# The second MLP's second layer as sign weights in float32r, with its own place in the order

## The chip, the cores and the metric

The kernel runs on one core of a Trainium2 chip. The metric is the device time of one execution in microseconds. The median of three runs before the change is 4103.9 us (4095.98 to 4111.07).

## The reference, cut to what matters

A two-layer transformer block works on `x` of 8 x 1024 x 256. The first layer has a windowed attention, a routed "heavy" attention and a small MLP; the second has a causal attention of 16 heads and an MLP with two-valued weights. The changed part is that last MLP, whose weights are replaced by their signs times a mean per output row:

```
def _binarize(w):
    alpha = jax.lax.stop_gradient(jnp.mean(jnp.abs(w), axis=1, keepdims=True))
    bw = alpha * jnp.sign(w)
    return w + jax.lax.stop_gradient(bw - w)
bw1 = _binarize(w1)                                   # 1024 x 256
h = jnp.einsum('bsd,hd->bsh', x, bw1) + b1
h = jax.nn.gelu(h, approximate=False)
bw2 = _binarize(w2)                                   # 256 x 1024
out = jnp.einsum('bsh,dh->bsd', h, bw2) + b2
```

Around it: `h = layernorm(x) * (1 + cb) + sb`, and `x = x + gb * out`.

## The kernel before, in words

The work goes batch by batch (`b`, 8 of them), and most stages by halves of a batch (`c`, 512 of the 1024 tokens). Each stage is written as a Python generator on each engine, and one list, `ORDER`, says whose step comes next; all engines follow that same list, each issuing its own instructions in order. `schedule()` makes the list from three lanes. Lane 0 holds `light` (windowed attention: 17 or 12 steps of QKV projections, then two steps for each of 16 units, and a tail) and `att` (the causal attention). Lane 1 holds `chain`, `heavy` and `mlp1`, lane 2 the other chains, `hrows` (row gathers for the heavy attention) and `hnorm`. `PACE` says how many steps of lane 0 go into one round, `SIDE` how many of a side lane, the constants after it (`HROWS_BEHIND_MLP` and so on) where a stage may begin, and `LAG` holds back `hnorm` and the first two chains.

`mlp1(b, c)` has 24 steps. Steps 0 to 7 are `norm_half`: statistics and normalisation on VectorE, a transposition on TensorE (L1471), and the split of the normalised input into two float32r parts, `hT2h` (ScalarE, L2322) and `hT2l`, the rest (VectorE, L1945). Steps 8 to 15 are the first layer, one block `m` of 128 hidden rows a step: two input blocks times two parts are four float32r matmuls of 512 columns against signs `w1s` (L1710, L1711), and ScalarE applies GELU with the block's mean `alpha1` as scale (L2442) into `g1`. Steps 16 to 23 are the second layer: for each of four token tiles, eight float32 matmuls with a tile of `g1` as stationary operand and `w2T` (256 columns) as moving one (L1724). Each of these float32 matmuls is two instructions in the trace. VectorE then multiplies by the gate (L2167) and GpSimd adds into `xt` (L2667). The signs of `w2` are multiplied by their means in the setup (VectorE and GpSimd).

First halves (`c = 0`) run beside the first steps of `att(b, 1)`, whose fills (L1568 to L1578 on TensorE) VectorE reduces (L2070 to L2078), and beside `hrows(b + 1)` (gathers L2501 on GpSimd, L1820 on VectorE). Second halves (`c = 1`) run beside `light(b + 1, 0)`, but for the last, which runs alone. In `light`, L1283 and L1287 are the QKV projections, L1774 and L2223 the masked scores and the exponentials, L1320 the turning of a unit. `exp_tables()` reloads ScalarE's table before an exponential when a GELU has been before it (L2180).

The lines that count most for the order:

```
if key[0] == "mlp1" and key[2] == 0 and n == 1 and not reached([(("att", key[1], 0), steps_of(("att", key[1], 0)))]):
    return
MLP1_BANKS = {0: (6, 7), 1: (7, 5, 6)}
```

## Time and profile before

| what | value |
|---|---|
| median of three runs | 4103.9 us |
| the profiled execution, its own time | 4090.72 us |
| its span, first to last instruction | 4089.0 us |
| TensorE busy | 3394.9 us, 83% |
| VectorE, ScalarE, GpSimd busy | 60%, 48%, 36% |
| mean granted TensorE clock | 0.911 |

The span is the stretch that the rows of the trace cover; the execution's own time has 1.7 us around it. Durations below are those of this execution, which lies 13.2 us under the median of the runs. An engine's busy share is taken over the whole span, in which stages with different limits follow each other eight times. A matmul's duration contains its latency, so the spacing of starts tells more than the mean duration.

### The profile page before, as it was taken

The numbers are of one execution on the slowest core, as the hardware profiler recorded it, in microseconds if no ns is written. First come the engines' busy times: TensorE is split into PE (matmuls) and PEld (weight loads), VectorE is DVE, ScalarE is ACT, GpSimd is POOL, SyncE is SP. The second block draws the span as 40 slices with busy tenths as digits, with TensorE's granted clock in tenths as the row PEclk, the third lists the DMA queues.
The fourth block names the chain that finished last, engine by engine and source line by source line (L and its number), as shares of the span: only waits on it lengthen the run. The fifth ranks groups of instructions, "written<-read, shape, count | busy, mean of one in ns | idle before, by whom it ended". The sixth has DMA issues, their size and how long they took to land. (4 is left out here: it accounts for less than half of the span.)

```text
span 4089.0 us, 81864 instructions
## 1 busy us (share of the span) xinstructions
PE 3394.9 (83%) x30905; PEld 2029.7 (50%) x30905; DVE 2463.2 (60%) x6188; ACT 1955.4 (48%) x4555; POOL 1478.4 (36%) x1799
## 2 busy tenths in 40 slices
PE   6368778897799878997798987998788977999787
PEld 2235554564446544565445544465444644456444
DVE  6755657367563666547573676637674465836662
ACT  5124445554364544554355543654445543655534
POOL 4123442244323542234422443235422344225411
PEclk8579789998899989998899988999899988999888
DMA  6210230002300122002400013002310024000220
GB/s 236 81 37 14 55 105 28 14 24 53 110 16 25 44 70 73 16 12 59 112 18 14 28 48 110 17 24 55 83 49 16 12 60 113 15 22 20 64 68 7
DMA packets 233604, 207.39 MB, mean 51 GB/s; under 512 B 13777, under 2 KB 214225, under 8 KB 233177
## 3 DMA queue, kind: packets, MB, share of 16 engines
q1 hardware_dynamic: 229168, 192.61, 16.7%
q0 software_dynamic: 3328, 8.39, 0.8%
q8 instruction: 252, 4.13, 0.4%
q14 instruction: 136, 1.11, 0.1%
q10 hardware_dynamic: 720, 1.15, 0.1%
HBM read 123.83 MB, written 77.69 MB: 49 GB/s over the span
## 5 line engine op out<-in xcount | busy, mean ns | idle before, releaser
L2399 ACT ACTIVATE arena<-pb 128x512 f32<-128x512 f32 (+3 forms) x1536 | 664.6, 492 | 239.5 <-PE pb L1615 232.2
L2479 POOL TENSOR_TENSOR arena<-arena,small 128x512 f32<-128x512 f32 x256 | 286.5, 1122 | 456.0 <-DVE small L1791 454.6
L2223 ACT ACTIVATE arena<-arena,small 128x256 f32<-128x256 f32 x512 | 255.8, 500 | 387.3 <-DVE small L1774 386.9
L1573 PE MATMUL pb<-arena 96*32 96x128 bf16 (+5 forms) x5280 | 372.4, 280 | 57.8 <-DVE arena L2078 23.7
L1615 PE MATMUL pb<-arena 98*32 98x512 bf16 (+3 forms) x4608 | 396.3, 339 | 28.1 <-ACT arena L2399 20.2
L1633 PE MATMUL pb<-arena,v 128*17 128x512 f32 (+3 forms) x3072 | 382.0, 499 | 24.1 <-POOL arena L2643 15.0
L2078 DVE TENSOR_REDUCE arena<-pb 128x1 f32<-128x512 f32 x512 | 333.1, 685 | 83.7 <-PE pb L1573 82.3
L2643 POOL TENSOR_SCALAR_AFFINE_SELECT arena<-arena 128x256 f32<-128x256 f32 x512 | 216.3, 426 | 461.1 <-ACT arena L2399 457.7
L1774 DVE CUSTOM_DVE_ANT_0 arena<-pb,wmask 128x256 f32<-128x256 f32 x512 | 195.8, 419 | 214.2 <-PE pb L1310 205.5
L1573 PEld LDWEIGHTS pb<-arena 96*32 96x32 bf16 (+1 forms) x5280 | 185.5, 102 | 246.9 <-issue 71.3
L1310 PE MATMUL pb<-arena 128*128 128x256 f32 x1024 | 280.3, 398 | 4.8 <-issue 3.6
L1287 PE MATMUL pb<-hTf,wqkv 128*128 128x512 f32 (+1 forms) x640 | 246.7, 537 | 24.4 <-DVE hTf L1743 11.5
L1724 PE MATMUL pb<-w2T,arena 128*128 128x256 f32 x1024 | 244.5, 391 | 10.8 <-ACT arena L2442 10.8
L1615 PEld LDWEIGHTS pb<-arena 98*32 98x32 bf16 x4608 | 138.5, 96 | 204.8 <-ACT arena L2399 108.6
L2349 ACT ACTIVATE arena<-arena,cols 128x256 f32<-128x256 f32 x256 | 148.5, 595 | 159.9 <-DVE arena L1988 158.1
L2070 DVE TENSOR_REDUCE arena<-pb 128x4 f32<-128x512 f32 x256 | 171.6, 688 | 84.9 <-PE pb L1573 82.4
L1724 PEld LDWEIGHTS pb<-w2T,arena 128*128 128x128 f32 x1024 | 196.6, 196 | 46.2 <-ACT arena L2442 14.5
L1310 PEld LDWEIGHTS pb<-arena 128*128 128x128 f32 x1024 | 187.1, 194 | 57.7 <-issue 26.1
L1320 PE MATMUL pb<-ident,arena 128*128 128x128 f32 x1024 | 161.4, 281 | 55.7 <-DVE arena L1784 34.3
L2539 POOL TENSOR_TENSOR arena<-arena,small 128x256 f32<-128x256 f32 x128 | 78.5, 613 | 348.2 <-DVE small L1886 348.1
L1578 PE MATMUL pb<-cmask,identb 128*32 128x512 bf16 (+1 forms) x640 | 120.0, 414 | 92.2 <-DMA arena<-split_k 56.0
L2072 DVE TENSOR_REDUCE arena<-pb 128x2 f32<-128x512 f32 x256 | 169.6, 686 | 26.8 <-PE pb L1573 26.4
(339 smaller groups left out, 7137.2 us busy)
## 6 DMA issues: line engine op xcount, KB each, us to landing
arena<-split_q SPq DMA_DIRECT2D x64, 384.0 KB, 3.8
arena<-split_k SPq DMA_DIRECT2D x24, 768.0 KB, 6.6
split_q<-arena SPq DMA_DIRECT2D x64, 192.0 KB, 2.1
split_q<-arena SPq DMA_DIRECT2D x96, 128.0 KB, 1.9
split_k<-arena SPq DMA_DIRECT2D x64, 192.0 KB, 2.2
split_k<-arena SPq DMA_DIRECT2D x96, 128.0 KB, 1.9
arena<-split_k SPq DMA_DIRECT2D x24, 384.0 KB, 8.2
xn<-h_d SPq DMA_DIRECT2D x8, 1024.0 KB, 9.3
```

Of the source, the lines that this page charges most:

```text
L1287: mm = t.matmul(bank[bk][:, 0:hi - lo], wqkv[:, k, col0:col0 + P], hT[:, k, lo:hi], start=k == 0, stop=k == KD - 1)
L1310: mm = t.matmul(bank[bk][:, j * 2 * P:(j + 1) * 2 * P], qt[:, p_, j, i * P:(i + 1) * P], kt[:, p_, i * P:i * P + 2 * P], start=True, stop= ...
L1573: mm = t.matmul(out[r:r + wide], qh[:, q0 + r:q0 + r + wide], kh_, **kw)
L1615: mm = t.matmul(bank[bk][r:r + 32, 0:w_], ka[slot(c, g)][0:KA, h, kt_ * P + r:kt_ * P + r + 32], qa[slot(c, g)][0:KA, h, q0:NH], start=Tru ...
L1633: t.matmul(bank[3][32 * h:32 * h + HD1 + 1, q0:NH], v1[:, kt_, G1 * g + h, :], pp[pn % 4][:, h % 2, 0:w_], start=kt_ == 0, stop=kt_ >= TH ...
L1724: mm = t.matmul(bank[bk][:, 0:D], g1[:, k, i * P:(i + 1) * P], w2T[:, k], start=k == 0, stop=k == FT - 1)
L1774: ins = v.tensor_tensor_reduce(out=sm[n % 2][:, j], in0=bank[n % 2][:, j * 2 * P:(j + 1) * 2 * P], in1=mk, scale=-1.0, scalar=3e38, op0=AL ...
L2078: ins = v.tensor_reduce(m[:, h, i, 3:4], bk, AX_X, ALU.max)
L2223: ins = s.activation(pm[n % 3][:, j], sm[n % 2][:, j], ACT.Exp, bias=nmx[:, 2 * sl + j:2 * sl + j + 1], scale=-1.0, accum_out=sml[:, 2 * s ...
L2399: s.activation(pp[pn % 4][:, h % 2, 0:w_], bank[n % 3][:, 0:w_], ACT.Exp).then_inc(a_exp1, 1)
L2479: g.tensor_tensor(pm[n % 3], pm[n % 3], rcl[:, 2 * sl:2 * sl + 2].unsqueeze(2).broadcast_to([P, 2, 2 * P]), ALU.mult).then_inc(p_norm0, 1)
L2643: g.affine_select(out=p2, in_=p2, pattern=[[0, 2], [1, P]], compare_op=ALU.is_ge, fill=0.0, base=0, channel_multiplier=-1).then_inc(p_tri, 1)
```

## The change

The second layer is computed like the first: signs as stationary operand in float32r, the activations as moving operand in two parts. GELU writes `gt`, two buffers of one block; VectorE copies it to float32r (`gh`) and subtracts the copy from it (`gl`). For each block `k` and each half `d` of the outputs there are two matmuls of 512 columns into two banks that collect all eight blocks (`MLP1_SUM`), so the output comes out transposed. ScalarE takes it out with the mean as scale (`moT`), TensorE turns it back by eight transpositions into two banks (`MLP1_TURN`), and VectorE's gate product and GpSimd's addition work on two token tiles at once. The second layer of block `m - 2` stands in the same step as the first layer of block `m`: after it in first halves, ahead of it in second halves. First-layer outputs of second halves have one bank (7) where there were three. The stage still has 24 steps. In the setup the signs of `w2` are no longer multiplied by their means. The order's constants change: `PACE`, `SIDE`, `HROWS_BEHIND_MLP`, `LAG`.

```
-PACE = {("light", 0): (1.88, 0.9, 0.9), ("light", 1): (1.0, 1.463, 1.1), ("att", 0): (1.461, 0.9, 0.9, 0.72), ("att", 1): (1.0, 1.15, 1.15, 0.632)}
+PACE = {("light", 0): (1.311, 0.9, 0.9), ("light", 1): (1.0, 1.463, 1.1), ("att", 0): (1.461, 0.9, 0.9, 0.72), ("att", 1): (1.0, 1.15, 1.15, 0.507)}
-        ("mlp1", 0): 1.0, ("mlp1", 1): 0.98, ("hrows", 0): 1.0, ("hnorm", 0): 1.0}
+        ("mlp1", 0): 0.99, ("mlp1", 1): 1.684, ("hrows", 0): 1.0, ("hnorm", 0): 1.0}
-HROWS_BEHIND_MLP, HEAVY_BEHIND_HROWS, HEAVY_BEHIND_ATT, HNORM_BEHIND_ATT, ATT_BEHIND_MLP, MLP_BEHIND_LIGHT = (6, 12, 11, 45, 13, 2)
+HROWS_BEHIND_MLP, HEAVY_BEHIND_HROWS, HEAVY_BEHIND_ATT, HNORM_BEHIND_ATT, ATT_BEHIND_MLP, MLP_BEHIND_LIGHT = (10, 12, 11, 45, 13, 2)
-LAG = 11
+LAG = 16
...
-                        v.wait_ge(b_alpha, 2 * m + 2)
-                        v.wait_ge(r_h[0], 16 * 2)
-                        v.scalar_tensor_tensor(out=wtmp[m % 2][:, 0:width], in0=sgn[:, c0:c0 + width], scalar=ac, in1=w, op0=ALU.mult,
-                                               op1=ALU.subtract).then_inc(b_sign, 1)
+                        v.tensor_copy(w, sgn[:, c0:c0 + width]).then_inc(b_add, 1)
                         yield
...
-                    g.wait_ge(b_sign, m - FT + 1)
-                    g.tensor_tensor(w, w, wtmp[m % 2][:, 0:width], ALU.add).then_inc(b_add, 1)
...
-        MLP1_BANKS = {0: (6, 7), 1: (7, 5, 6)}
+        MLP1_NORM, MLP1_W1, MLP1_SUM, MLP1_TURN = ({0: (6, 7), 1: (7, 5)}, {0: (6, 7), 1: (7,)}, {0: (0, 1), 1: (5, 6)}, {0: (6, 7), 1: (7, 5)})
...
+                    def second(k):
+                        if k == 0:
+                            for bk in sums:
+                                for w in left[bk]:
+                                    t.wait_ge(*w)
+                                left[bk] = None
+                        t.wait_ge(gl_set, FT * H + k + 1)
+                        for d in range(KD):
+                            t.matmul(bank[sums[d]], w2s[:, k, d * P:(d + 1) * P], gh[:, k % 3], start=k == 0, stop=False)
+                            mm = t.matmul(bank[sums[d]], w2s[:, k, d * P:(d + 1) * P], gl[:, k % 3], start=False, stop=k == FT - 1)
+                        mm.then_inc(t_w2, 1)
+
+                    for m in range(FT + 2):
+                        if m < FT and c == 0:
+                            first(m)
+                        if m >= 2:
+                            second(m - 2)
+                        if m < FT and c == 1:
+                            first(m)
+                        yield
+                    for d in range(KD):
+                        left[sums[d]] = [(a_mo, KD * H + d + 1)]
+                    yield
+                    for u in range(2):
+                        bk = MLP1_TURN[c][u]
                         for w in left[bk]:
                             t.wait_ge(*w)
-                        for k in range(FT):
-                            if i == 0:
-                                t.wait_ge(a_g, FT * H + k + 1)
-                            mm = t.matmul(bank[bk][:, 0:D], g1[:, k, i * P:(i + 1) * P], w2T[:, k], start=k == 0, stop=k == FT - 1)
...
+                        t.wait_ge(a_mo, KD * H + KD)
+                        for i in range(2):
+                            for d in range(KD):
+                                mm = t.transpose(bank[bk][:, (KD * i + d) * P:(KD * i + d + 1) * P], moT[:, d, (2 * u + i) * P:(2 * u + i + 1) * P], ident[:, :])
+                        mm.then_inc(t_mo, 1)
...
+                    for m in range(FT + 2):
+                        k = m - 1
+                        if 0 <= k < FT:
+                            v.wait_ge(a_g, FT * H + k + 1)
+                            if k >= 3:
+                                v.wait_ge(t_w2, FT * H + k - 2)
+                            v.tensor_copy(gh[:, k % 3], gt[:, k % 2]).then_inc(gh_set, 1)
+                        if 0 <= k < FT:
+                            v.wait_ge(gh_set, FT * H + k + 1)
...
+                            v.tensor_tensor(gl[:, k % 3], gt[:, k % 2], gh[:, k % 3].bitcast(F32), ALU.subtract).then_inc(gl_set, 1)
+                        yield
...
+                        v.tensor_tensor(xadd2[u], bank[MLP1_TURN[c][u]].rearrange("p (t d) -> p t d", t=2), gates[:, 3].unsqueeze(1).broadcast_to([P, 2, D]),
+                                        ALU.mult).then_inc(v_w2, 1)
...
+                            s.wait_ge(t_w1, FT * H + m + 1)
+                            if m >= 2:
+                                s.wait_ge(gl_set, FT * H + m - 1)
+                            gelu_tables[0] = True
+                            s.activation(gt[:, m % 2], bank[MLP1_W1[c][m % len(MLP1_W1[c])]], ACT.Gelu, scale=alpha[:, m:m + 1],
+                                         bias=cols[:, C_FB1 + m:C_FB1 + m + 1]).then_inc(a_g, 1)
+                        yield
+                    s.wait_ge(t_w2, FT * (H + 1))
+                    s.wait_ge(gl_set, FT * (H + 1))
+                    for d in range(KD):
+                        s.activation(moT[:, d], bank[MLP1_SUM[c][d]], ACT.Copy, scale=alpha[:, FT + d:FT + d + 1]).then_inc(a_mo, 1)
```

## Rows read from the trace of the kernel before

**Rows 1.** The page's part 1: busy us, share of the span, instructions of each engine.
```profile
PE 3394.9 (83%) x30905; PEld 2029.7 (50%) x30905; DVE 2463.2 (60%) x6188; ACT 1955.4 (48%) x4555; POOL 1478.4 (36%) x1799
```

**Rows 2.** Groups by line and form, TensorE: count, busy us, mean ns, idle before.
```profile
L1724 PE MATMUL pb<-w2T,arena 128*128 128x256 f32 x1024 | 244.5, 391 | 10.8 <-ACT arena L2442 10.8
```

**Rows 3.** Windows, a first half: length, busy PE, PEld, DVE, ACT, POOL, PEclk, DMA.
```profile
1526.00:1563.00 37.00, 30.98 (x134) 23.54 (x135) 14.69 (x34) 9.44 (x12) 16.07 (x16) 0.84 0.68 181
```

**Rows 4.** Windows: a second half, and the mean over all seven.
```profile
1724.00:1771.00 47.00, 42.15 (x191) 30.90 (x190) 11.92 (x45) 30.95 (x54) 8.41 (x9) 0.96 0.00 1
...
sum 322.00, PE 288.53 PEld 213.62 DVE 83.11 ACT 199.23 POOL 58.72; mean PE 41.22 PEld 30.52 DVE 11.87 ACT 28.46 POOL 8.39
```

**Rows 5.** Waits of TensorE in the first half, 1526 to 1563 us.
```profile
PE pb L1471 <- DVE arena L1933: 6.3, 1, 6.3
PE pb L1578 <- DVE arena L2070: 2.5, 1, 2.5
PE pb L1710 <- DVE hT2l L1945: 2.3, 1, 2.3
```

**Rows 6.** Waits of TensorE in the second half, 1724 to 1771 us.
```profile
PE pb L1710 <- ACT arena L2442: 2.4, 2, 1.8
PE pb L1724 <- ACT arena L2442: 2.4, 1, 2.4
```

**Rows 7.** Timeline of the first half: gathers, their readers, second layer's first two tiles.
```profile
1528.97 1.08 POOL L2501 DMA_INDIRECT arena<-h_d,idx_all  x1 [3.79 <-PE pb L1471]
...
1544.22 0.42 DVE L1820 CUSTOM_DVE_ANT_0 arena<-arena 128x256 f32<-128x256 f32 x1 [4.34 <-DMA arena<-h_d,idx_all]
...
1546.56 4.54 PE L1724 MATMUL pb<-w2T,arena 128*128 128x256 f32 x16
...
1551.38 3.62 PE L1724 MATMUL pb<-w2T,arena 128*128 128x256 f32 x16
```

**Rows 8.** Timeline of the second half: a table load and what waits behind it.
```profile
1737.26 1.28 ACT L2442 ACT_TABLE_LOAD   x1
...
1738.55 1.45 ACT L2442 ACTIVATE arena<-pb,cols,alpha 128x512 f32<-128x512 f32 x2
1739.38 0.65 PE L1710 MATMUL pb<-hT2h,w1T 128*128 128x512 f32 x1 [1.83 <-ACT arena L2442]
```

**Rows 9.** ScalarE's groups by line and form: GELU's and exponentials' table loads.
```profile
L2442 ACT ACT_TABLE_LOAD x38 | 48.8, 1283 | 24.1 <-PE pb L1711 23.6
L2180 ACT ACT_TABLE_LOAD x37 | 47.5, 1283 | 60.2 <-PE pb L1615 34.2 <-DVE small L1879 25.5
L2232 ACT ACTIVATE arena<-pb 128x512 f32<-128x512 f32 x128 | 74.0, 578 | 60.5 <-PE pb L1320 60.5
```

**Rows 10.** Timeline of the last half, full clock: starts of neighbouring float32r matmuls; second layer.
```profile
4061.44 0.39 PE L1711 MATMUL pb<-hT2l,w1T 128*128 128x512 f32 x1
4061.67 0.40 PE L1710 MATMUL pb<-hT2h,w1T 128*128 128x512 f32 x1
...
4065.01 14.08 PE L1724 MATMUL pb<-w2T,arena 128*128 128x256 f32 x64
```

**Rows 11.** Timeline: eight transpositions of 128x128 float32 in a row.
```profile
1711.13 1.04 PE L1260 MATMUL pb<-ident,xn 128*128 128x128 f32 x8
```

**Rows 12.** VectorE's groups by line and form.
```profile
L2078 DVE TENSOR_REDUCE arena<-pb 128x1 f32<-128x512 f32 x512 | 333.1, 685 | 83.7 <-PE pb L1573 82.3
L2167 DVE TENSOR_TENSOR arena<-pb,gates 128x256 f32<-128x256 f32 x64 | 27.2, 425 | 170.8 <-PE pb L1724 138.3 <-issue 32.6
L1945 DVE TENSOR_TENSOR hT2l<-arena,hT2h 128x512 fp32r<-128x512 f32 x32 | 22.5, 707 | 1.4
L1992 DVE TENSOR_TENSOR arena<-pb,gates 128x512 f32<-128x512 f32 x32 | 22.1, 692 | 37.7 <-PE pb L1512 37.7
L845 DVE CAST arena<-arena 128x256 f32<-128x256 bf16 x8 | 2.3, 288 | 0.0
L994 DVE COPY arena<-arena 128x128 f32<-128x128 f32 x1 | 0.2, 218 | 0.0
```

110 lines of the change are left out of this document (49 added, 61 removed).

## The prediction

> **What bounds the kernel now.** I read the page's busy shares first: TensorE is busy 83% of the span, VectorE 60%, ScalarE 48%, GpSimd 36% [rows 1]. No engine is full, but TensorE is the one to which stages come back, so work taken off it counts where it is the last wait. Then I looked where the changed stage stands. It appears in 16 clusters: eight first halves of some 37 us beside the first fills of the causal attention, seven second halves of some 46 us beside the next batch's QKV projections and first attention units, and one second half alone at the end. The windows show that they are bounded differently. In a first half TensorE is busy 31.0 of 37 us, VectorE only 14.7, and the granted clock is 0.84 [rows 3]: part of it runs at 1.2 GHz, behind a 6.3 us wait for the norm [rows 5]. In the second halves TensorE is busy 288.5 of 322 us and ScalarE 199.2 [rows 4].
>
> The waits name what the rest is. In a first half TensorE waits 2.3 us for the split of the input and 2.5 us in a fill for VectorE [rows 5]; VectorE itself then stood in its queue before a gather's landing (4.34 us, L1820) [rows 7]. In a second half both waits of 2.4 us go to the GELU [rows 6], and the timeline shows why: GELUs alternate with the attention's exponentials, each change loads a table for 1.28 us, and TensorE stands 1.83 us for the bank behind it [rows 8]. Both loads together are there 75 times [rows 9], some 8 in each of the seven second halves.
>
> **The change: array work.** The old second layer is 64 instructions a half (1024 over 16 halves [rows 2]), 14.08 us at 2.4 GHz, so 0.22 us each [rows 10]. The new one is 8 blocks x 2 outputs x 2 parts = 32 float32r matmuls of 512 columns. The first layer has that form already; neighbouring ones start 0.23 us apart [rows 10], so 7.4 us. The eight transpositions of the result cost 1.0 us [rows 11]. Net -5.7 us a half, at full clock.
>
> **VectorE and ScalarE.** Eight subtractions a half are like L1945, 0.71 us [rows 12]. The copy of 128x512 float32 to float32r in SBUF is not in the trace. Copies inside SBUF took 0.218 us for 128 elements and 0.288 for 256 [rows 12]; that line gives 0.43 at 512. The other bound is one element a cycle like the subtraction, 0.71. I take 0.43, since the nearest rows are copies too. Four gate products of 0.425 become two of 0.692 [rows 12]. VectorE gets 8 x 1.14 + 1.4 - 1.7 = 8.8 us more a half (11 with the dear copy), 141 us in all, 60% to 63 or 64%. ScalarE takes out two banks more, 0.58 us each [rows 9].
>
> The Trainium skill (SBUF — State Buffer, on the port pair that VectorE and GpSimd share) says that such a copy locks the pair and that GpSimd cannot write a gather's descriptors meanwhile. No row here shows that lock; it speaks against the change, and it is a rival below.
>
> **First halves.** A step of both layers is 8 matmuls, 1.86 us, and a fill of about 0.5 us beside it; VectorE has 0.43 + 0.71 + 0.69 for the fill's reduction [rows 12], 1.83 us, and 2.3 in the steps with a gathered row. So TensorE still ends last, barely. Worked out with the new constants, the order has `hrows` begin four mlp steps later, and its readers on VectorE at mlp steps 14 to 17 and not 10 to 13, while GpSimd still issues the gathers right behind its bias addition. They have landed then, so the 2.5 us wait goes, and with it the dip of the clock behind it: the first tile at L1724 took 4.54 us, the next 3.62 [rows 7], so 0.9. What is late next: second(0) waits for GELU, copy and subtraction of block 0 (1.0 us after the steps at hand), VectorE and TensorE share the pace for eight steps (0.2 each, 1.6), and the transpositions wait for `moT` (0.9, ScalarE's two copies less the fills between). Sum: -5.7 - 2.5 - 0.9 + 3.5 = -5.6 us. Bounds -7.5 (no new wait) and -2.5 (the dear copy and a wait of 0.6 us in each step). `heavy` still begins after attention step 11, and VectorE's scaling of the gathered rows is done just before, which I cost at nothing; if late it is 1 us.
>
> **Second halves.** By the order all eight GELUs now stand beside QKV steps 8 to 15, whose evacuations need no exponential. So no alternation: the 4.8 us of waits go [rows 6], and the 1.9 us that a clock of 0.96 takes out of 47 us [rows 4]. With the array work that is -12.4 us. Back come these. The norm's steps are pressed between QKV steps 2 and 7, so the split is late by 1.2 us (its 2.3 us chain [rows 5] less the QKV step that covers it). First-layer blocks 0 and 1 follow each other with one bank and no second layer between: one table load and one GELU, 1.28 + 0.78, and the semaphores, 2.3 us [rows 8]. In later steps TensorE's second(m - 1), 0.93 us, covers GELU(m - 1), 0.78 with its semaphores, but for 0.1; 1.0 in all. `moT` stands on ScalarE behind the evacuation of QKV step 16, which waits for TensorE, while TensorE is already at the transpositions: 0.2 + 0.6 + 1.2 = 2.0 us. Behind these transpositions on TensorE stands `light` step 17, so the attention units wait as well. Last, the first attention units lose the mlp matmuls that covered their softmax: 1.2 us. Sum of these 7.7, net -4.7 us. Bounds: -9 (half of them hidden) and -1.5 (1 us in each of three more steps).
>
> The Trainium skill (ScalarE: Activation LUTs, what a table load costs) has 2.66 us for a switch, with a drain. Here the GELU starts 1.29 us after the load [rows 8], so the trace decides; by the page the one bubble would be 1.4 us longer in each second half, some 10 us in all.
>
> **The last half** is alone. With one bank a step is first layer, GELU, next first layer: 0.93 + 0.78 + 0.3 = 2.0 us, 16 for eight, where it was 7.5 + 14.1 = 21.6 behind each other, and its tail is longer by 4 us: -1.5 us (+2 to -3). The setup loses two small products on VectorE and two on GpSimd beside the token selection; I cost it at nothing. `LAG` 16 moves the first two chains and every `hnorm` by a few steps; `hnorm` now ends at attention step 70 of 77, some 8 us of TensorE's work before it is needed, which covers it.
>
> **Sum.** 8 x -5.6 = -45, 7 x -4.7 = -33, -1.5: -79 us against the execution of 4090.7, so 4012, a factor of 0.981. On the median of 4103.9 it is 4025.
>
> **The rivals.**
> - More comes: the new waits mostly hide, -7.5 and -9 a half: 8 x 7.5 + 7 x 9 + 3 = 126, so 3978. For it speaks that the profile shows slack on ScalarE; against, that a queue in program order rarely hides all.
> - VectorE sets the pace: the dear copy and steps of 2.6 us in first halves, the chain late in second ones: 8 x 2.5 + 7 x 1.5 - 2 = 28, so 4075.
> - GpSimd is locked out (the skill's rule as a mechanism here): each pair of copy and subtraction, 1.1 us, can hold back one of the four gathers, up to 4.5 us, and the readers stall VectorE's queue with the copies behind it. Half of the first halves' gain goes: +22 us, 4047. The wait of 4.34 us [rows 7] speaks for a sore spot, the four steps' delay against it.
> - No change: what TensorE gains in the halves is waited for at `heavy` and the chains, where VectorE ends last. Within 20 us of 4104. Little speaks for it, as nothing there depends on a fixed time.
> - Slower, by one mechanism: one step's links run in series, because VectorE's copy stands behind an evacuation that waits for TensorE. Then a step in second halves is 0.93 + 1.0 + 0.43 + 0.71 + 0.93 = 4.0 us for 1.86, +21 us a half for the -12.4 gained. In second halves alone that is 7 x 21 - 7 x 12.4 - 45 = +15; in first halves too, whose gain without new waits is 9.1 us, it is 15 x 21 - 87 - 73 = +155. I put it between, +85, at 4189. It decides from (87 + 45) / 70 = 1.9 us of wait in each step of second halves. Against it: second(m - 2) lies two steps behind its first layer.
>
> **Chances.** My forecast 0.56 (own range 4000 to 4052), more 0.14, GpSimd 0.09, VectorE 0.10, no change 0.05, slower 0.06. The range for 8 in 10 is 3985 to 4075: it leaves out the lower part of "more", and the last two. Half a per cent, about 20 us, is what a measurement can tell from no change. Faster 0.89, same 0.05, slower 0.06.
>
> **What would show it.** In the profile after: L1724's group gone, the new float32r pair at 0.23 us spacing; the SBUF copy at 0.43 us; table loads down from 77 to some 33; no gather wait on VectorE in first halves; first halves near 30.5 us; TensorE busy some 90 us less, VectorE some 140 more; a wait of about 2 us before the second halves' transpositions. Wrong would be: copies of 0.7 us, TensorE waiting for `gl` in most steps, or halves that are shorter while the time between them grows.

## The result, and the profile after

The changed kernel takes 4079.28 us (median; 4075.96 to 4080.89) beside 4095.98 us (4087.93 to 4111.07) for the kernel before in the same comparison: a ratio of 0.994, with a 95% interval of 0.9921 to 0.9958. A second measurement (e1) gave 0.9932 (0.991 to 0.9954). It is faster, but by 17 to 27 us where 79 were forecast, and it lies just outside the forecast's range of 3985 to 4075.

The page of the changed kernel, its head and part 1 (busy us, share of the span, instructions):

```profile
span 4075.6 us, 81566 instructions
...
PE 3334.5 (82%) x30521; PEld 1944.0 (48%) x30521; DVE 2603.0 (64%) x6412; ACT 1924.3 (47%) x4543; POOL 1470.0 (36%) x1765
```

Against [rows 1] VectorE has 139.8 us more, as forecast (141). TensorE's busy time fell by 60 us where some 90 had been forecast; what became of the rest stands below the table. The prices of the new layer's single instructions are right. Groups of the changed kernel by line and form (VectorE: subtraction, copy, gate product, scaled gathered rows; TensorE: the second layer's pair; ScalarE: the table loads before GELUs and before exponentials):

```profile
L2179 DVE TENSOR_TENSOR gl<-arena,gh 128x512 fp32r<-128x512 f32 x128 | 94.4, 738 | 4.4
L2174 DVE CAST gh<-arena 128x512 fp32r<-128x512 f32 x128 | 55.2, 432 | 120.7 <-ACT arena L2470 107.3 <-issue 13.0
L2188 DVE TENSOR_TENSOR arena<-pb,gates 128x512 f32<-128x512 f32 x32 | 21.3, 682 | 11.0 <-PE pb L1736 11.0
L1843 DVE TENSOR_SCALAR arena<-arena,small 128x256 f32<-128x256 f32 x32 | 18.0, 567 | 0.3
...
L1714 PE MATMUL pb<-gh,w2T 128*128 128x512 f32 x256 | 118.2, 462 | 7.2 <-DVE gl L2179 6.8
L1715 PE MATMUL pb<-gl,w2T 128*128 128x512 f32 x256 | 104.3, 407 | 0.0
...
L2470 ACT ACT_TABLE_LOAD x16 | 20.5, 1283 | 40.4 <-PE pb L1702 40.4
L2204 ACT ACT_TABLE_LOAD x15 | 19.2, 1283 | 63.2 <-PE pb L1606 24.0 <-DVE small L1890 22.9 <-DVE small L1785 16.2
```

The copy takes 0.432 us (0.43 taken), the subtraction 0.738 (0.71). With two loads in the setup there are 33 table loads (33 forecast; 77 before [rows 9]). GELUs no longer alternate with exponentials.

So the pieces are as forecast, and the time isn't. To see where it went I cut every batch at the same four instructions in both traces: **second-half stretch**, from the next batch's first transposition to its 13th attention unit; **untouched stretch**, from there to the norm's first transposition of the first half, in which no changed instruction stands; **first-half stretch**, from there to the first score of `att(b, 1)`'s heads, so the mlp with what follows it, `heavy`'s beginning; and the rest of the batch. Sums over the profiled executions, in us; e3 is an experiment below, the kernel before with nothing changed but the order's constants:

| stretch | before | e3 | after | forecast for the change | measured |
|---|---|---|---|---|---|
| up to batch 0's first transposition | 236.1 | 235.8 | 231.9 | 0 | -4.2 |
| batch 0 without its first half | 441.0 | 436.8 | 437.1 | 0 | -3.9 |
| eight first-half stretches | 588.7 | 569.5 | 572.7 | -45 | -16.0 |
| seven second-half stretches | 567.9 | 559.2 | 557.8 | -33 | -10.1 |
| seven untouched stretches | 1512.4 | 1529.3 | 1528.6 | 0 | +16.2 |
| seven rests | 693.7 | 693.3 | 695.1 | 0 | +1.4 |
| last half | 49.3 | 49.0 | 52.4 | -1.5 | +3.1 |
| span | 4089.0 | 4072.9 | 4075.6 | -79 | -13.4 |

The profiled execution of the kernel before (4090.7 us) lies below the median of its runs in every comparison (4096 to 4106), so the table shows 13.4 of the 17 to 27 us. A part of that is in the untouched stretches, which are as short as 1512.4 us in no other trace (e6, below).

Windows over the seven first-half stretches of batches 1 to 7, the sum line (length, busy us of each engine, mean of one), first of the kernel before:

```profile
sum 511.90, PE 417.47 PEld 236.40 DVE 292.01 ACT 133.51 POOL 148.24; mean PE 59.64 PEld 33.77 DVE 41.72 ACT 19.07 POOL 21.18
```

The same of e3, the old layer in the new order:

```profile
sum 494.42, PE 410.39 PEld 231.50 DVE 290.82 ACT 133.51 POOL 145.84; mean PE 58.63 PEld 33.07 DVE 41.55 ACT 19.07 POOL 20.83
```

The same of the changed kernel:

```profile
sum 497.36, PE 387.85 PEld 197.05 DVE 358.77 ACT 142.56 POOL 144.46; mean PE 55.41 PEld 28.15 DVE 51.25 ACT 20.37 POOL 20.64
```

From e3 to after, TensorE's busy time falls by 3.2 us a half and its idle time grows by 3.6 (length less busy: 70.6 - 58.6 = 12.0, then 71.1 - 55.4 = 15.6). The same happens in the seven second-half stretches: busy 73.7 to 69.9, idle 6.2 to 9.8. The busy time that the new layer takes off TensorE comes back as waiting, and it is less than the 5.7 us forecast. Two second-half stretches with the full clock throughout (1.00) show how much less; batch 3 of e3, then batch 2 of the changed kernel (length, busy of PE, PEld, DVE, ACT, POOL, granted clock, DMA share, GB/s):

```profile
1699.99:1775.84 75.85, 72.15 (x345) 49.44 (x344) 27.99 (x97) 33.20 (x77) 24.01 (x25) 1.00 0.10 32
1216.12:1293.24 77.12, 67.91 (x322) 43.77 (x320) 36.52 (x111) 34.61 (x79) 23.64 (x23) 1.00 0.10 32
```

That is 4.2 us and not 5.7: without the second layer's own matmuls TensorE's busy time in these two is 59.0 and 60.6 us, so the other ones show 1.6 us more. Why isn't shown. The rest of what is missing is the clock: of a first-half stretch 11.6 us are lost to it in e3 and 14.4 after (length times what the mean granted clock lacks to 1).

The waits of TensorE in one first-half stretch (batch 2; us in total, times, longest), before; those for the norm and the split are in [rows 5]:

```profile
PE pb L1578 <- DVE arena L2070: 3.1, 2, 2.5
PE pb L1573 <- DVE arena L2078: 3.0, 2, 2.8
```

The second of these in e3 (L1578 is down to 0.6 there):

```profile
PE pb L1573 <- DVE arena L2078: 3.3, 2, 2.8
```

And in the changed kernel, where L1578 is L1569 and L1573 is L1564:

```profile
PE pb L1462 <- DVE arena L1944: 6.3, 1, 6.3
PE pb L1564 <- DVE arena L2089: 5.4, 3, 2.3
...
PE pb L1701 <- DVE hT2l L1956: 2.4, 1, 2.4
PE pb L1736 <- ACT arena L2476: 1.0, 1, 1.0
PE pb L1569 <- DVE arena L2081: 0.6, 1, 0.6
```

The 2.5 us wait behind the gather is gone, as forecast (L1578 3.1 to L1569 0.6), and e3 shows that the order did that. But the other wait for the fills' reductions grew from 3.0, and 3.3 in e3, to 5.4, so that TensorE waits for reductions as long as before, 6.0 us for 6.1. VectorE's timeline there, in the changed kernel (start, us, line, operation), shows what they stand behind:

```profile
1546.30 0.68 DVE L2188 TENSOR_TENSOR arena<-pb,gates 128x512 f32<-128x512 f32 x1
1546.90 0.26 DVE L1840 TENSOR_SCALAR small<-small 128x4 f32<-128x4 f32 x1
1547.19 1.31 DVE L1843 TENSOR_SCALAR arena<-arena,small 128x256 f32<-128x256 f32 x1
1548.42 0.68 DVE L2089 TENSOR_REDUCE arena<-pb 128x1 f32<-128x512 f32 x1
...
1550.97 0.91 DVE L1851 MEMSET arena<- 64x1024 f32 x1 [0.16 <-issue]
1552.14 0.91 DVE L1852 MEMSET arena<- 64x1024 f32 x1 [0.25 <-issue]
```

A gate product, the norm of the gathered rows and a scaled row stand in VectorE's queue ahead of a reduction (L2089 at 1548.42), for which TensorE waits 2.3 us. It waits 0.8 us for the reduction before it (1545.70), which stands behind the other gate product, and 2.2 us behind `heavy`'s two memsets. Only the first two waits are new: before, the scaled rows and all gate products but the last lay beside the old second layer, in which VectorE waited for TensorE, but the memsets stood behind it then too, with a wait of 2.8 us. Two rows of VectorE's timeline before, a gate product with the idle time ahead of it in brackets, and the first memset:

```profile
1562.81 0.42 DVE L2167 TENSOR_TENSOR arena<-pb,gates 128x256 f32<-128x256 f32 x1 [2.27 <-PE pb L1724]
...
1564.36 0.91 DVE L1840 MEMSET arena<- 64x1024 f32 x1 [0.53 <-issue]
```

### The profile page after: what moved, and what is told of

The parts are those of the page before. It is cut to its first block and busy times, and to the rows that moved or that the text cites. A ratio compares the mean times of both kernels' runs of the same rounds, so it can differ in the third digit from the quotient of the medians.

```text
span 4075.6 us, 81566 instructions
## 1 busy us (share of the span) xinstructions
PE 3334.5 (82%) x30521; PEld 1944.0 (48%) x30521; DVE 2603.0 (64%) x6412; ACT 1924.3 (47%) x4543; POOL 1470.0 (36%) x1765
## 3 DMA queue, kind: packets, MB, share of 16 engines
q1 hardware_dynamic: 229168, 192.61, 16.9%
## 5 line engine op out<-in xcount | busy, mean ns | idle before, releaser
L1564 PE MATMUL pb<-arena 96*32 96x128 bf16 (+5 forms) x5280 | 381.3, 280 | 78.1 <-DVE arena L2089 41.8
L2089 DVE TENSOR_REDUCE arena<-pb 128x1 f32<-128x512 f32 x512 | 335.4, 684 | 94.1 <-PE pb L1564 91.6
L1564 PEld LDWEIGHTS pb<-arena 96*32 96x32 bf16 (+1 forms) x5280 | 184.9, 101 | 273.9 <-DVE arena L2089 84.9
L1278 PE MATMUL pb<-hTf,wqkv 128*128 128x512 f32 (+1 forms) x640 | 258.8, 551 | 30.8 <-DVE hTf L1754 19.1
L1278 PEld LDWEIGHTS pb<-hTf,wqkv 128*128 128x128 f32 x640 | 117.9, 200 | 145.7 <-issue 121.0
L1569 PE MATMUL pb<-cmask,identb 128*32 128x512 bf16 (+1 forms) x640 | 119.4, 412 | 77.8 <-DMA arena<-split_k 59.6
L1311 PEld LDWEIGHTS pb<-ident,arena 128*128 128x128 f32 x1024 | 118.9, 142 | 130.8 <-ACT arena L2256 54.5
```

What stands on the lines that cost most here:

```text
L1278: mm = t.matmul(bank[bk][:, 0:hi - lo], wqkv[:, k, col0:col0 + P], hT[:, k, lo:hi], start=k == 0, stop=k == KD - 1)
L1311: mm = t.transpose(bank[2][:, j * P:(j + 1) * P], pm[n % 3][:, j // 2, (j % 2) * P:(j % 2 + 1) * P], ident[:, :])
L1564: mm = t.matmul(out[r:r + wide], qh[:, q0 + r:q0 + r + wide], kh_, **kw)
L2089: ins = v.tensor_reduce(m[:, h, i, 3:4], bk, AX_X, ALU.max)
```

## The experiments

Each ratio is to the kernel before, with its 95% interval; the changed kernel for comparison is e1 (0.9932). "Stretches" are those of the table, as means of batches 1 to 7.

**e1, the changed kernel again.** No edit.

> The changed kernel once more, as the base of this group and to see how far one stretch differs between two executions of the same program. Theory V (the gain of the first halves is given back to VectorE's queue at their end, that of the second halves to new waits on ScalarE): the stretch from the norm's transpositions to the first attention score is again 71 us and the one from the next batch's first transposition to its 13th attention unit 79.7 us on average, each within 1 us. Theory C (the loss is a chance of TensorE's clock in that one execution): these means move by 2 us or more. The ratio to the kernel before is 0.994.

Measured: 4075.14 us, 0.9932 (0.991 to 0.9954). Its stretches repeat those of the table within 0.5 us each (first halves 71.4 for 71.1, second 79.2 for 79.7, untouched 218.0 for 218.4, means of seven), as theory V had it. Where an experiment below leaves a kind of stretch alone, its mean lies between 70.8 and 71.4 us in first halves and between 79.2 and 80.2 in second ones; a difference inside these bounds says nothing.

### Order and layer apart

**e2, the new layer in the old order.** **e3, the old layer in the new order.**

```
e2: -PACE = {("light", 0): (1.311, ...  +PACE = {("light", 0): (1.88, ...   (all the constants back)
e3: the same constants, the other way, in the kernel before
```

> The new layer in the old order: PACE, SIDE, HROWS_BEHIND_MLP and LAG as they were. Theory V: the layer alone gives the second halves nothing, because GELUs and exponentials alternate again, and with them VectorE's copies; some 10 table loads a half return, so some 25 us slower than the changed kernel, near 4100. Rival (the order is what costs, by pressing the steps together): faster than the changed kernel, 4060 or less.

> The kernel before with the new order's constants alone (PACE, SIDE, HROWS_BEHIND_MLP, LAG); its second layer stays float32. Theory: a good part of what the change gained in second halves is the order's, since it puts all eight GELUs beside QKV steps, so that they no longer alternate with exponentials. That is worth up to 4.8 us a half, 34 us; the shifts in the stretch that holds no instruction of the change cost 2.3 us a batch, 16; the start gains 9, and the last half has nothing of it. Sum -27: about 0.993 to 0.996 of the kernel before. Rival: this order only suits the new layer's steps (in it the old second layer's 14 us stand beside the units of attention, which wait behind them): slower than before by 0.3% or more, and the change's gain is the layer's.

Measured: e2 4124.66 us, 1.0052 (1.0035 to 1.0069): slower than before. Theory V's direction came, at twice its size: it has 77 table loads again, and its second-half stretches are 86.5 us (81.1 before, 79.7 after). e3 4075.16 us, 0.9927 (0.9907 to 0.9946): the same as the whole change. This is the main finding. The new layer alone is a loss of half a per cent in the old order, the order alone is the whole gain, and beside the new order the layer is worth nothing that can be measured. e3's expectation named the direction and, nearly, the size.

The table above then splits the change. The order gives 19.2 us in the first halves, 8.6 in the second ones, and takes 16.9 in the untouched stretches. The layer gives 3.9 in the setup, where its products of signs and means are gone, 1.4 in the second halves, and costs 3.2 in the first and 3.4 in the last (and 1.4 in the parts between: 2.7 in all). Each number is one execution against another; how far the one on the untouched stretches holds is e6's question.

**e6, the old order for the untouched stretch alone**, in the changed kernel.

```
+ for b in range(1, B):
+     (a, z) = places of light(b, 0) step 41 and of mlp1(b, 0) step 1
+     out[a:z] = older[a:z]
```

> The changed kernel with the old order from attention unit 12 of light(b, 0) to the start of mlp1(b, 0), for b from 1 to 7; there no instruction of the change stands, only the order differs by single steps. That stretch is 216.1 us before and 218.4 after on average. Theory O (the new constants shift the chains by a step there, and that costs 2.3 us a batch): back to 216 us, some 14 us less in all, ratio 0.990. Rival (it is TensorE's clock, which falls differently when what comes before has another length): the stretch stays at 218 us and the time within 5 us of the changed kernel, ratio 0.993.

Measured: 4070.91 us, 0.9921 (0.9899 to 0.9944); the interval overlaps e1's. Batch by batch the untouched stretches are 219.5, 214.9, 217.4, 217.4, 213.1, 219.4, 215.4 us, with the kernel before at 217.0, 214.5, 217.4, 218.9, 212.9, 219.2, 212.6 and the changed one at 215.8, 221.6, 219.8, 215.5, 214.5, 216.2, 225.1. The new constants move the steps of the untouched stretch too, and by this pair 11.5 of its 16.2 us come back with the old places. The other traces make it less. Thirteen kernels here have the new places with nothing added there (after, e1, e3, e4, e5, e7, e9, e10, e11, e13, e14, e15, e17), and the seven stretches sum to 1519.8 to 1529.3 us, 1523.6 in the mean; five have the old places (before, e2, e6, e12, e18), with 1512.4 to 1524.2, 1518.9 in the mean. So the new places cost some 5 us, and the 16.2 of the table is mostly a short execution beside a long one. In single batches the places are clear: batch 7 takes 221.0 to 226.0 us with the new ones and 212.5 to 215.5 with the old, batch 2 217.5 to 221.8 and 214.5 to 216.0, but batch 6 213.3 to 217.3 and 218.1 to 220.0.

### What holds the first halves

**e4 and e5, less work for TensorE**: the matmuls on `gl` left out, in first halves (e4) or second halves (e5). The low part of the activations is then missing from the output.

```
-  t.matmul(..., gh[:, k % 3], start=k == 0, stop=False)
-  mm = t.matmul(..., gl[:, k % 3], start=False, stop=k == FT - 1)
+  mm = t.matmul(..., gh[:, k % 3], start=k == 0, stop=k == FT - 1)
```

> In first halves the 16 matmuls with the second part (gl) are left out, VectorE's copy and subtraction stay. 3.7 us of TensorE's work less in each of eight halves. Theory V: VectorE's queue ends the stretch, so less than 1.5 us a half, 0 to 12 us in all. Rival (TensorE still bounds the first halves): 3.5 us a half, 28 us in all.

> In second halves the 16 matmuls with the second part (gl) are left out, VectorE's work stays. Theory V: TensorE bounds these halves but for a few fixed waits, so most of the 3.7 us comes, 20 to 26 us over the seven halves beside the projections. Rival (the chain of GELU, copy and subtraction paces the steps): under 8 us.

Measured: e4 4062.08 us, 0.9903 (0.9883 to 0.9924); e5 4065.66 us, 0.9906 (0.9884 to 0.9929). 16 matmuls of 0.23 us are 3.7 us a half. Of them 1.6 arrived in the first-half stretches (71.05 to 69.47) and 1.35 in the second (79.69 to 78.34), between the two theories in both. Some 40% of the work that was taken off arrived, where the sum had all of it on the path. What became of the rest differs. In first halves it isn't waited for: TensorE's idle time is 15.6 us as in the changed kernel, but 16.9 us are lost to the clock and not 14.4. In second halves idle time grew by 0.8 us and the loss to the clock by 1.0.

**e7, ScalarE makes the copies to `gh` in first halves**, VectorE the subtractions only.

```
+ if c == 0:
+     s.activation(gh[:, m % 3], gt[:, m % 2], ACT.Copy).then_inc(gh_set, 1)
```

> In first halves ScalarE makes the copy gh, right behind each GELU, and VectorE only the subtraction: 8 x 0.43 = 3.4 us less on VectorE. Theory V (VectorE's queue ends the first halves): 1.5 to 3 us a half, 12 to 24 us in all, ratio 0.988 to 0.990. Theory K (TensorE's clock takes back what is gained): under 1 us a half, with more of the half at the lower clock.

Measured: 4069.74 us, 0.992 (0.9897 to 0.9943). VectorE has 4.0 us less in a first-half stretch, and the stretch is 0.6 shorter (70.44). That is theory K's size without its reason, since 13.8 us are lost to the clock beside 14.4.

**e14, less work for VectorE**: the subtraction cut to two columns, both matmuls of a pair read `gh`. **e15, both**: that subtraction, and no second matmul. Both leave out the low part.

```
-  v.tensor_tensor(gl[:, k % 3], gt[:, k % 2], gh[:, k % 3].bitcast(F32), ALU.subtract)
+  v.tensor_tensor(gl[:, k % 3, 0:2], gt[:, k % 2, 0:2], gh[:, k % 3, 0:2].bitcast(F32), ALU.subtract)
```

> The changed kernel with VectorE's subtraction cut to two columns and both matmuls of a pair reading gh (left out: the low part of the activations). TensorE's work is unchanged, VectorE has 5.2 us less in each half, 83 in all. Theory A, VectorE's queue took TensorE's place: 2 to 3 us less in each half, 4037 (0.984 of the kernel before). Theory B, TensorE and its clock set the halves: under 0.7 us a half, 4067 to 4077. Removing TensorE's 3.7 us instead gave 1.6 us a first half and 1.4 a second one (e4, e5).

> The changed kernel without the subtraction (as e14) and without the matmuls on the low part (as e4 and e5 together), so VectorE has 83 us less and TensorE 56 us less. Theory A, the two queues guard each other (either one alone gives back what the other loses): more than e4 + e5 + e14 together, so 4077 - 13 - 10 - 40 - 15, about 4000 or less. Theory B, something outside the layer's own work sets the halves (the norm's chain ahead of them, the readers of the gathered rows, the clock): less than e4 + e5 + e14 together, 4030 to 4050.

Measured: e14 4070.06 us, 0.9905 (0.9882 to 0.9927); e15 4029.13 us, 0.9805 (0.9781 to 0.983). In e14 the first-half stretches are as long as before the edit (71.02 for 71.05) though VectorE has 4.7 us less in each: TensorE's idle time fell by 0.7 us, and 0.8 more were lost to the clock. In e15 they are 67.48, that is -3.6, where e4 alone gave -1.6 and e14 nothing. By the ratios e15 takes 52 us less than e1 (0.9932 - 0.9805, of 4100), and e4, e5 and e14 together 34. The intervals are too wide to prove the difference from the totals; e15's first-half stretch is shorter than e4's in six of the seven batches. That is more than the sum of the parts, as theory A wants it, though the time is the one that theory B named (4030 to 4050). But the reason of theory A, that each queue guards the other, isn't in the trace: TensorE's idle time in a first-half stretch is 15.3 us in e15 and 15.6 in e4 and in the changed kernel. What e15 has beyond e4 is the clock, with 14.8 us lost to it beside 16.9. Why it was higher isn't shown. And the 5.4 us wait for the reductions is still there; TensorE's waits in e15's first-half stretch of batch 2:

```profile
PE pb L1462 <- DVE arena L1943: 6.3, 1, 6.3
PE pb L1564 <- DVE arena L2088: 5.4, 3, 2.3
```

So that wait isn't made by the layer's copies and subtractions. It belongs to the work that now follows the mlp, as e9 shows.

**e9, the old place of the gathered rows** (`HROWS_BEHIND_MLP` 6 and not 10, in the changed kernel).

> HROWS_BEHIND_MLP back to 6 alone, so the readers of the gathered rows and their scaling stand four mlp steps earlier in VectorE's queue. Theory V: 2 to 3 us of VectorE's work leave the end of the first half, 10 to 20 us faster than the changed kernel. Rival (the gathers have not landed by then and VectorE's copies stand behind the wait): 1 to 4 us a half slower, 10 to 30 us in all.

Measured: 4085.41 us, 0.9957 (0.9942 to 0.9972), slower than e1 if anything. Three of the four scaled rows are done inside the mlp again, where the changed kernel has none, and the wait is smaller (batch 2, 5.4 in the changed kernel, 3.3 in e3):

```profile
PE pb L1564 <- DVE arena L2089: 3.8, 3, 2.0
```

So the new part of the wait comes for the most part from the place of the rows, but the time doesn't. TensorE's idle time in the first-half stretches fell by 1.6 us, and they grew by 0.9: 2.3 us more were lost to the clock. The rival's mechanism shows in batch 1 alone, where VectorE waited 5.0 us for a gather (79.0 us for 75.3); the six others grew by 0.4.

**e17, `heavy`'s memsets made by GpSimd**, out of VectorE's queue.

```
-  v.memset(qz[0:DH, :, 1], 0.0)
-  v.memset(qz[DH:P, :, 0], 0.0)
+  g.memset(qz[:, :, 1], 0.0).then_inc(v_hset, 1)
+  g.memset(qz[:, :, 0], 0.0).then_inc(v_hset, 1)
```

> The changed kernel with heavy's two memsets (0.91 us each on VectorE, ahead of the reductions for which TensorE waits 2.24 us in each first half) made by GpSimd, which is idle there, over all 128 partitions. Theory, VectorE's queue keeps the end of the first halves: 1 to 2 us less in each of seven, 4062 to 4070 (0.991 of the kernel before). Rival, the place is taken by what stands behind them (the scaled rows, slow beside GpSimd; TensorE's own transpositions for heavy): within 4 us of the changed kernel, 4073 to 4081.

Measured: 4071.59 us, 0.9933 (0.991 to 0.9955): the rival, by the ratio. The memsets' wait was there before the change too, so this relieves VectorE, but not of what the change moved. Waits of TensorE, 1500 to 1575 us (it was 5.4 there too in the changed kernel):

```profile
PE pb L1564 <- DVE arena L2087: 4.0, 3, 2.3
```

The sum line of its seven first-half stretches:

```profile
sum 496.78, PE 400.05 PEld 195.40 DVE 357.46 ACT 144.20 POOL 156.59; mean PE 57.15 PEld 27.91 DVE 51.07 ACT 20.60 POOL 22.37
```

The wait is 1.4 us shorter and idle time falls by 1.8 a stretch (15.6 to 13.8), but TensorE is busy 1.7 longer with the same instructions, at a lower granted clock (15.9 us lost to it beside 14.4). The length is 70.97 for 71.05.

### The clock

**e8 and e16, matmuls of no use in TensorE's waits for the norm.** e8: 20 ahead of the norm's transpositions. e16: 28 there, and 10 between them and the first layer.

```
+ for _ in range(28):
+     t.matmul(bank[banks[0]], identb[:, :], cmask[...], start=True, stop=True)
...
+ t.wait_ge(a_nx, H + 1)
+ for _ in range(10):
+     t.matmul(bank[MLP1_NORM[0][0]], identb[:, :], cmask[...], start=True, stop=True)
```

> Before the norm's transpositions of first halves, in the 6.3 us in which TensorE waits for VectorE, 20 bfloat16 matmuls of 512 columns on constants, whose result is overwritten. They add 4.3 us of work at 2.4 GHz to a wait, and nothing else. Theory K: the clock stays up, the first 13 us of each first half run at twice the speed, 3 to 4 us a half less, 25 to 30 us in all, ratio near 0.986. Theory V: the time from the transpositions on is set by ScalarE and VectorE, so within 5 us of the changed kernel, or slower where the added matmuls run at the lower clock and end after the norm.

> The changed kernel with 28 matmuls of no use ahead of the norm's transpositions of each first half and 10 more between them and the first layer, so that both waits for the norm are covered (e8 left 2.0 and 2.6 us open, and the clock fell). Theory, the clock is a cause: the 20 first-layer matmuls at 0.43 us come down to 0.23 us, 3 to 4 us less in each of seven first halves, 4054 (0.988 of the kernel before). Rival: what TensorE gains by the clock it waits for VectorE in the same half: S within 5 us of the changed kernel, 4072 to 4082. Third: the clock falls in spite of the work and the time stays or rises.

Measured: e8 4078.87 us, 0.9945 (0.9922 to 0.9968). Waits of 2.0 and 2.6 us stayed open behind the 20 matmuls, and the first layer still ran at the lower level. e16 4073.65 us, 0.9936 (0.9907 to 0.9964). Timeline of the first layer in batch 2, the changed kernel:

```profile
1519.23 0.80 PE L1701 MATMUL pb<-hT2h,w1T 128*128 128x512 f32 x1 [2.42 <-DVE hT2l L1956]
1520.25 0.63 PE L1701 MATMUL pb<-hT2h,w1T 128*128 128x512 f32 x1
1521.11 0.63 PE L1701 MATMUL pb<-hT2h,w1T 128*128 128x512 f32 x1
```

The same in e16, from the ten added matmuls on:

```profile
1518.77 2.33 PE L1702 MATMUL pb<-cmask,identb 128*128 128x512 bf16 x10 [0.43 <-ACT arena L2351]
1521.65 0.50 PE L1710 MATMUL pb<-hT2h,w1T 128*128 128x512 f32 x1 [0.54 <-DVE hT2l L1965]
1521.99 0.39 PE L1711 MATMUL pb<-hT2l,w1T 128*128 128x512 f32 x1
1522.21 0.40 PE L1710 MATMUL pb<-hT2h,w1T 128*128 128x512 f32 x1
```

In the changed kernel the L1701 instructions, with one L1702 between two of them, start 0.86 us apart, so 0.43 a matmul: 1.2 GHz. In e16 neighbours start 0.23 apart: 2.4 GHz, from the first on. Windows of the mlp and of the 21 us behind it (length, busy of PE, PEld, DVE, ACT, POOL, granted clock, DMA share, GB/s), changed kernel:

```profile
1516.00:1545.00 29.00, 24.43 (x101) 17.04 (x99) 17.64 (x36) 10.71 (x14) 12.56 (x12) 0.79 0.84 210
1545.00:1566.00 21.00, 14.73 (x84) 4.41 (x83) 15.05 (x25) 2.28 (x5) 3.75 (x3) 0.76 0.19 62
```

The same windows in e16:

```profile
1519.00:1546.00 27.00, 22.55 (x108) 14.69 (x106) 19.07 (x39) 9.57 (x13) 12.76 (x13) 1.00 0.93 231
1546.00:1567.00 21.00, 15.17 (x84) 4.42 (x84) 14.94 (x25) 2.87 (x6) 3.22 (x3) 0.76 0.18 62
```

The whole mlp now has the full clock, yet the first-half stretches are only 0.6 us shorter (70.44). In its timeline TensorE waited 1.3 us for the first GELU where it was 0.5, and the part behind the mlp took 43.0 us in the mean and not 42.2. So the lost clock in the mlp isn't what holds these halves: the rival of e16. The clock behind the mlp wasn't tested by it, since that part has 0.76 in both. The 21 us behind the mlp in the kernel before:

```profile
1563.00:1584.00 21.00, 16.57 (x112) 5.14 (x110) 14.64 (x24) 4.68 (x10) 3.35 (x4) 0.92 0.19 63
```

Over batches 1 to 7 the part behind the mlp loses 6.1 us to the clock before, 6.8 in e3, 9.3 after, and 10.5 in e16. No run has the full clock there.

### Second halves and the table loads

**e10, ScalarE's tables early**, in both halves.

```
+ if m == 0:
+     s.preload_act_table_set("gelu_and_others")
  s.wait_ge(t_w1, FT * H + m + 1)
...
  s.activation(moT[:, d], ...)
+ exp_tables()
```

> The changed kernel; ScalarE loads the GELU's table before it waits for the first layer's block 0, and the exponential's table right behind its two copies of the sums, in both halves. Theory: in second halves TensorE's wait of 2.2 us behind block 0 loses the load's 1.28, and the wait of 1.8 us as the attention units begin goes for the most part; in first halves 0.5 us or less is saved. 7 x 2.3 + 8 x 0.4 = 19 us less, 4058 (0.989 of the kernel before). Rival: the loads are hidden or the waits are set by the evacuation ahead of the GELU on ScalarE, so that the same wait is there without the load: within 5 us of the changed kernel, 4072 to 4082.

Measured: 4041.08 us, 0.9845 (0.9826 to 0.9865), twice the expected gain. Waits of TensorE in a second half (the one of [rows 4] before), the changed kernel:

```profile
PE pb L1701 <- ACT arena L2470: 2.2, 1, 2.2
PE pb L1736 <- ACT arena L2476: 1.9, 1, 1.9
PE pb L1311 <- POOL arena L2511: 1.8, 1, 1.8
```

The same in e10:

```profile
PE pb L1736 <- ACT arena L2478: 1.9, 1, 1.9
PE pb L1701 <- ACT arena L2472: 1.5, 1, 1.5
...
PE pb L1311 <- POOL arena L2514: 0.5, 1, 0.5
```

Two waits are 0.7 and 1.3 us shorter, and the second-half stretches 1.55 (78.14). The first-half ones are 2.0 shorter (69.07): the wait for the first GELU (0.5) is gone, and one for ScalarE at `heavy`'s projections (L1236) fell from 2.5 to 1.4. The untouched ones are 1.3 shorter and the rests 0.7, some 14 us in all, half of which is less time lost to the clock (1.0 us a batch). The other half isn't placed, and the untouched ones' part is no more than they differ by from trace to trace. The Trainium skill (ScalarE: Activation LUTs, rules for kernel authors) budgets 2.7 us for every switch to a different set and says to do all of one set before switching. The grouping is what the new order did; that a switch also costs where the groups stay as they are, and can be put where ScalarE is waiting anyway, is what e10 adds. The price doesn't agree: in the rows a load is 1.28 us and the GELU starts 1.29 us after its beginning [rows 8], so 1.3 us a switch is what this case has.

**e13, e3 with the early tables**: the old layer, the new order.

> The kernel before (old float32 second layer) with the new order's constants and the early table loads of e10. It differs from e10 by the new layer alone. Theory: the layer is worth nothing once the order is given, with the loads early or not: e3's 4075 less e10's 36, about 4040, 0.9845 of the kernel before, within 8 us of e10. Rival: the loads hid the layer's gain (in the new layer the second layer's matmuls wait for each GELU, in the old one they come eight steps later), and here the early loads are worth under 15 us: 4060 or more, so that the layer is worth 20 us beside e10.

Measured: 4049.84 us, 0.986 (0.9835 to 0.9886), beside e10's 0.9845 (0.9826 to 0.9865): the layer is worth 6 us or nothing here, as the theory had it. Its gain wasn't hidden behind the loads.

**e11, ScalarE takes the sums out before it evacuates QKV step 16**, in second halves (its `yield` behind the last GELU is skipped).

> The changed kernel; in second halves ScalarE's two copies of the sums stand ahead of its evacuation of QKV step 16, not behind it. Theory (the prediction's term of 2.0 us for moT, 1.94 in the trace): 1.5 to 1.9 us less in each of seven second halves, 10 to 13 us, 4065. Rival: TensorE's next steps wait for the evacuation, which now comes later, and the gain is under 4 us.

Measured: 4067.93 us, 0.9903 (0.9885 to 0.9922). The wait for `moT` of 1.9 us is gone from its trace, but its second-half stretches are 79.84 for 79.69: idle time is 0.7 us less, the clock took 1.0 more, and the profiled span only 2.4 us less. The total suggests a gain of 12 us and the trace doesn't show it; the profiled execution (4074.89 us) is the longest of the four. It stays open.

**e12, e6 + e7 + e10 + e11. e18, e6 + e10 + e11 + e17.**

> Four edits together: the old order's stretch between the first attention units and the norm of the first halves (e6), ScalarE's copies to gh in first halves (e7), the early tables and the sums taken first. Theory: each takes another wait, so they add up: -8 - 9 - 19 - 11 = -47, about 4030, 0.982 of the kernel before. Rival: they share waits (ScalarE's queue in first halves bears the copies and the early loads; a wait taken from TensorE comes back at the next queue): half of it, 4053, 0.988.

> e12 without ScalarE's copies to gh and with the memsets of e17: early table loads, the sums taken first, the old stretch of the order, the memsets on GpSimd. Theory: the loads and VectorE's queue are two waits, so e17's gain comes on top of e12's 4043: about 4032, 0.982 of the kernel before. Rival: they are one wait in the first halves, and it stays at e10's and e12's time, 4038 to 4046 (0.984 to 0.986).

Measured: e12 4042.67 us, 0.9841 (0.9825 to 0.9858); e18 4031.55 us, 0.9842 (0.9819 to 0.9865). All that was added to e10 (0.9845) can't be told from nothing. So e12's waits are shared, as its rival says, at a time between its two numbers (0.982 and 0.988). e18 has the ratio of its rival and the time of its theory (4032), and its interval holds both: it doesn't decide. Both, like e10, beat the changed kernel and the one before.

## Why the prediction was wrong

The prices of single instructions and most of the mechanisms were right; what failed is the step from the pieces to the path. Four terms of the sum carry it: the order's gain in second halves, the array work of -5.7 us in first halves, the untouched stretch at nothing, and the clock as a pure gain. Split into order and layer by e3, its terms stand so (us for one half; measured: means of batches 1 to 7):

| | forecast | measured |
|---|---|---|
| first half, order: gather wait -2.5, clock -0.9 | -3.4 | -2.5 |
| first half, layer: array -5.7, new waits +3.5 | -2.2 | +0.4 |
| second half, order: waits -4.8, clock -1.9, late split +1.2 | -5.5 | -1.2 |
| second half, layer: array -5.7, bubble 2.3, chain 1.0, `moT` 2.0, cover 1.2 | +0.8 | -0.2 |

**The second halves' order part** is the dearest miss: 7 x 4.3 = 30 us. The waits for the alternating GELUs did go, but in their place came other ones, in some batches. e3's second-half stretches are 79.7, 82.7, 75.8, 78.3, 83.0, 83.0, 76.6 us, where the kernel before had 80.1 to 82.7. Waits of TensorE in e3's second-half stretch of batch 3, a short one:

```profile
PE pb L1287 <- DVE hTf L1743: 1.4, 1, 1.4
PE pb L1320 <- ACT arena L2232: 1.0, 3, 0.4
```

And of batch 5, a long one:

```profile
PE pb L1287 <- DVE hTf L1743: 3.8, 1, 3.8
PE pb L1710 <- DVE hT2l L1945: 2.3, 1, 2.3
```

Where neither is late, 5.3 us arrived (81.2 to 75.8; the sum without its late split has 6.7); where both are, 4.7 us went to them (3.8 - 1.4 + 2.3). The late split was in the sum with 1.2 us everywhere; the wait for `hTf` wasn't in it. Which batches have it can be read from `ORDER`: in batches 2, 5 and 6 the new list puts step 3 of the mlp, VectorE's first two normalised tiles (L1933), ahead of step 4 of `light`, which begins with the copy to `hTf` (L1743), and the wait is 3.3, 3.8 and 3.8 us; in 1, 3, 4 and 7 step 3 comes behind it, and the wait is 1.4, 1.4, 2.2 and 2.2. In batch 5 VectorE stands 1.2 us at L1933 for GpSimd with the copy behind it. e13 has the same order and the same pattern (79.7, 81.6, 75.8, 76.7, 83.2, 83.3, 76.6 us). The changed kernel has the same waits in the same batches.

**The second halves' layer part** agrees with its forecast (+0.8, -0.2) by luck. Its terms were -5.7 of work and +6.5 of waits, and measured are -3.8 and +3.6 in the mean: both too large. The block-0 bubble (2.2) and `moT` (1.9) came as summed, the chain of 1.0 us didn't.

**The untouched stretch was costed at nothing**, as the same work in the same time. In this pair of executions it cost 16.2 us, over all traces of both orders some 5, with 9 more in batch 7 and 3 to 4 less in batches 1 and 6 (e6). The prediction had worked out that `LAG` moves every `hnorm` and the first two chains by a few steps, and called them covered. The cover was looked for in one place (the deadline of `hnorm`) and not along the 217 us in which the steps stand.

**The first halves' layer part** missed by 8 x 2.6 = 21 us. The new waits were summed at 3.5 us and TensorE's idle time grew by 3.6, so the term that failed is the array's: of -5.7 us on the path -3.2 came as busy time. Some 1.5 us are missing at the full clock too, by the second halves above, and the rest is the lower clock under the new layer (14.4 us lost for 11.6), for which the sum had no term.

Nor are the waits the ones that were summed. "TensorE still ends last, barely" was true inside the mlp, where idle time grew by 1.5 us (0.6 for block 0, 1.0 for `moT`). From the norm's first transposition to the mlp's last instruction the first halves took 28.8 us, where e3 had 32.8 (means of seven), in part because three fills slipped behind it. From there to the end of the stretch they took 42.2 and not 37.9, and the sum had nothing for that part: the three fills, 2.1 us more of idle time, and 9.3 us lost to the clock for 6.8. The sentence that failed there is "VectorE's scaling of the gathered rows is done just before, which I cost at nothing; if late it is 1 us". The new order alone had put two of the four scaled rows behind the mlp; the new layer put all four there, with both gate products and three reductions, and the wait is 5.4 us where e3 has 3.3. For this work the old layer's 14 us were cover.

That explains the wait, and not the length. With the rows in their old place the wait is 3.8 us, and the part behind the mlp is still 42.1 (e9); with the memsets gone it is 4.0, and the part is 42.6 (e17). In both the granted clock behind the mlp was lower (11.4 us lost to it). And batch 7, which has no gathered rows and no `heavy` behind its first half, went from 50.7 us in e3 to 50.0: the layer brought 0.7 of its 2.2 us even there. Whether VectorE's queue or TensorE's clock holds the part behind the mlp stays open; no run has the full clock in it.

**The clock** was taken as a gain of 0.9 and 1.9 us and was a loss: in the first-half stretches 14.4 us of 71.1 were lost to it, 11.8 of 73.1 before, and 2.4 in the second-half ones, 1.7 before. The 1.9 was read from one second half (0.96 in [rows 4]) and is more than a whole second-half stretch lost in the mean. Inside the mlp the clock isn't the bound (e16), but it took back what e9 and e17 saved in waits and what e4 saved in work. What sets how much it gives in a stretch stayed open.

**The setup** was costed at nothing and gave 3.9 us. **The last half** was 3.4 us longer with the new layer, not 1.5 shorter. Its tail is 4.3 us longer, as the sum had it (4). Its steps took 2.1 us each, also as summed (2.0), but the sum counted eight of them, 16 us. From first to last matmul of the two layers it is 23.2 us: block 0 alone takes 4.3 with its table load and GELU, two steps of the second layer stand behind the eighth, and the first blocks ran at 1.2 GHz. Before, the same is 24.4.

**The rivals.** "GpSimd is locked out" didn't happen: the gathers' issues took 1.02 us in the mean beside 1.10 before, and no reader waits for one. e3 has 1.02 too, so the layer's copies and subtractions changed nothing there. The sore spot showed on VectorE: three of its 128 subtractions took 2.3 us and not 0.7, each beside a gather and two products of GpSimd. "VectorE sets the pace" came nearest in its number, 4075, but by another way: not the dear copy, not 2.6 us steps, but VectorE's other work without its cover, and a lower clock. "No change" had a part of the mechanism in one half-sentence, that what TensorE gains "is waited for at `heavy`", with a chance of 0.05; batch 7 shows that it isn't the whole. "Slower by a serial chain" didn't happen.

Of what was to show it: the pair at 0.23 us spacing, the copy at 0.43, 33 loads, no gather wait, 1.94 us ahead of the second halves' transpositions all came; TensorE's 90 us less came as 60. "Halves that are shorter while the time between them grows" was named as the sign that it would be wrong, and it is what the trace shows (halves 26 us shorter, untouched stretches 16 longer in this pair).

## What to carry to other kernels

Before work is taken off the busiest engine, ask what the other engines do beside it: if they use its time as cover, TensorE can wait for them at the next thing they own. Look at the granted clock beside the waits: where work (e4) or waits (e9, e17) were taken out of the first halves, 1.5 to 2.5 us came back as a lower clock. A change that comes with new constants for the order is two changes; price the order's part over the whole of every stretch whose steps it moves, batch by batch, since one list can place the same steps differently in each, and run each part alone (e2, e3) before explaining their sum. A table load that stands behind the wait for its first input can be put ahead of that wait, and here that was worth some 36 us, beside 27 for the new layer and the new order together.
